# A table held in two float32r parts instead of three bf16 parts, with shared places for the 0/1 tiles, in the attention pass of a graph network kernel

## The chip, the core and the metric

The kernel is one launch on one NeuronCore of a Trainium2 chip. The metric is device time of the whole launch in microseconds. A difference of about 0.5% (some 98 us) is what a measurement of this kernel can tell from no change.

## The reference, cut to what matters

Four graph layers follow each other on 6250 nodes and 200000 edges. The edges are sorted by `dst`. The second layer is the one the change is in: for each edge it looks up the rows of both ends, makes one attention number of them, and sums and takes the maximum of the weighted rows over the edges of each node.

```python
row, col = (edge_index[0], edge_index[1])          # src, dst
ef = edge_label @ trans_weight
node_feat = x[row] * x[col]
att = jax.nn.sigmoid(_leaky_relu(node_feat @ attention_weight) + _leaky_relu(ef @ edge_attention_weight))
wef = ef * att
wnf = x[col] * att
wsf = x[row] * att
...
s = jax.ops.segment_sum(vals, idx, num_segments=n)
mx = jax.ops.segment_max(vals, idx, num_segments=n)
```

## The kernel before, in words

All engines are programmed by hand with semaphores; there is no scheduler. Edges lie as 128 partitions times 1568 places, and a pass walks over them in blocks of B = 16 places (2048 edges). A loop of IT = 49 turns handles two such blocks, called halves: `h` is 0 or 1, `n = 2 * i + h` counts them, and buffers that come in pairs are indexed by `h`. So the attention pass (`attention_pass`, lines 1143 to 1487) does 98 halves.

In each half the row `x[src]` of 16 x 128 edges is needed. Ten of the sixteen come by indirect DMA from the DRAM table `att_table` into `rows[h]` (POOL, L1263). The other K = 6 are looked up on TensorE: the table of 6272 nodes, 65 numbers each, stands in SBUF as 128 partitions x 7 classes (`WIDE_CLASSES`) x 455 columns. `one_lo[h]` is a 0/1 tile that says in which partition and class an edge's node is, made by VectorE from `keys[h]` in `one_hots` (L1367, 7 instructions for 7 classes of 768 columns). For each of the six places TensorE multiplies the table's 7 classes by that 0/1 tile and adds up in PSUM (`multiply`, L1341). Because the 0/1 tile and the table are bf16, the float32 table is split in three bf16 parts whose sum is the number: 7 classes x 3 parts = 21 matmuls of 455 columns for a place, 42 for one call of `multiply(h, g)`, which does two places (G = 3 groups g = 0, 1, 2). VectorE then picks the right one of 7 slots in `pick(g)` (L1404) and adds up in `gather(g)` (L1407).

The order in a half `n` is written out:

- TensorE: `multiply(h, 0)` after pick 1 of half n - 1, `multiply(h, 1)` after pick 2 of half n - 1, the label products (L1357), `multiply(h, 2)` after pick 0 of half n. There are two PSUM tiles `p_slots`, used in turn.
- VectorE: pick 0, the 0/1 tiles of the next half (`one_hots`, `one_slots`), gather 0, the 16-step chain that completes `xdst` (L1427), pick 1, label score, gather 1, pick 2, gather 2, product with `x[dst]` and reduction to the score (L1446 to L1457), rows for the attention (L1461, L1462), then `chains` for the half before (L1383, L1385): 16 steps of running sums and running maxima in `run`.
- ScalarE: sigmoid of the score (L1326), then three times 16 weighted rows (L1302): first `out_rows`, then two parts of `msg`.
- POOL: 16 scatters of `out_rows` to the DRAM tensor `sent` (`scatter`, L1272) when VectorE and ScalarE have made them, and behind them in the same queue the 10 gathers of a later half (`gather`, L1263). The order is gather of half n + 1, scatter of n, gather of n + 2, scatter of n + 1. So after each scatter of half n come the gathers of half n + 2.
- SyncE: loads of `xdst`, labels and keys for later halves, and the store of `run` to `running_dst` (`store_last`, L1224).

Ahead of the pass the table is split by `split_wide` (L852, L854) on VectorE while POOL scatters `begun_x` (L1133). The last layer (`softmax_pass`, L1630) has the same kind of lookup, but from a table in two float32r parts, with `e_one_lo` tiles in float32r (L1777 and L1800); it is not changed. Lines below are those of the kernel before.

## Time and profile before

| | us |
|---|---|
| median of 3 runs | 19641.05 (19631.51 to 19712.04) |
| span of the profiled execution | 19593.6 |
| first and last sigmoid of the attention pass | 5940.0 and 10831.2 |
| PE busy in the span | 11895.5 (61%) |
| DVE busy | 10634.3 (54%) |
| POOL busy | 9080.8 (46%) |
| ACT busy | 4354.8 (22%) |

The profile is one execution. PE is TensorE's matmul, PEld its weight load, DVE VectorE, ACT ScalarE, POOL GpSimd, SP SyncE. "Idle before" is time in which an engine stood idle just ahead of an instruction; "issue" as its reason means that the engine waited for nothing that the profile shows. No engine is busy all the time: the attention pass, about a quarter of the span, has to be read by what follows what.

### The profile page before, as it was taken

How to read it: one execution, taken by the hardware profiler on the slowest of the kernel's cores; microseconds unless marked ns; L12 is line 12 of the kernel's file. 1: busy time of each engine (PE TensorE's matmuls, PEld its weight loads, DVE VectorE, ACT ScalarE, POOL GpSimd, SP SyncE). 2: the span in 40 equal slices, each digit the busy share in tenths (PEclk: the TensorE clock that was granted, in tenths of full speed). 3: DMA queues.
4: the chain of work that ended last, by engine and by line, in shares of the span. 5: the costliest groups of instructions: out<-in, count | busy, mean ns of one | idle time of the engine just before them, and what ended most of it. 6: DMA issues, size and time to landing. Idle time of an engine off the chain costs nothing. (4 is left out here: it accounts for less than half of the span.)

```text
span 19593.6 us, 235897 instructions
## 1 busy us (share of the span) xinstructions
PE 11895.5 (61%) x70205; PEld 7895.5 (40%) x70205; DVE 10634.3 (54%) x24515; ACT 4354.8 (22%) x14847; POOL 9080.8 (46%) x9348
## 2 busy tenths in 40 slices
PE   4444445555546666666666446776776777566664
PEld 3333334444432222222222115665664333355453
DVE  5555545555544545555545794554554555356565
ACT  2333322333312222222222330000000111022221
POOL 4444434444445455455455103555444555444444
PEclk7777767777767777777777667887887888678777
DMA  2111112222212222222222671111111111022221
GB/s 62 58 58 58 58 48 75 77 76 76 77 55 64 69 65 70 69 65 70 69 65 70 214 260 31 32 32 29 31 32 29 34 34 34 23 56 57 58 56 48
DMA packets 637409, 1245.55 MB, mean 64 GB/s; under 512 B 206034, under 2 KB 390391, under 8 KB 586531
## 3 DMA queue, kind: packets, MB, share of 16 engines
q1 hardware_dynamic: 322624, 912.21, 13.3%
q0 software_dynamic: 300160, 269.02, 7.8%
q10 hardware_dynamic: 14337, 61.82, 0.8%
q14 instruction: 270, 2.20, 0.0%
q8 instruction: 18, 0.29, 0.0%
HBM read 475.84 MB, written 768.08 MB: 63 GB/s over the span
## 5 line engine op out<-in xcount | busy, mean ns | idle before, releaser
L1030 PE MATMUL p_slots<-part,one_lo 128*128 128x208 bf16 (+1 forms) x27048 | 3678.2, 296 | 1143.2 <-issue 992.4
L1341 PE MATMUL a_p_slots<-att_part,a_one_lo 128*128 128x455 bf16 x12348 | 2986.2, 389 | 1868.8 <-issue 1782.6
L1030 PEld LDWEIGHTS p_slots<-part,one_lo 128*128 128x128 bf16 x27048 | 2663.8, 105 | 2157.5 <-issue 1446.8
L990 POOL DMA_INDIRECT rows<-gcn_table,index x2450 | 2384.7, 973 | 2462.5 <-DVE p_msg L1109 1507.9
L1341 PEld LDWEIGHTS a_p_slots<-att_part,a_one_lo 128*128 128x128 bf16 x12348 | 1254.1, 102 | 3623.5 <-issue 2574.9
L1272 POOL DMA_INDIRECT sent<-a_out_rows,a_place x1568 | 1543.2, 984 | 2165.6 <-DVE a_run L1383 1688.3
L556 POOL DMA_INDIRECT msg<-x_rows,index x1372 | 1310.7, 955 | 1431.8 <-ACT index L574 1020.1
L1078 DVE TENSOR_TENSOR picked<-p_slots,one_hi 128x832 f32<-128x832 f32 (+1 forms) x588 | 708.2, 1204 | 2280.1 <-remote 1825.8
L556 POOL DMA_INDIRECT msg<-h_rows,index x1274 | 1225.8, 962 | 1533.0 <-ACT index L574 1174.2
L622 PE MATMUL p_slots<-x_part,key_lo 128*128 128x448 f32 x6916 | 1859.9, 429 | 121.6 <-DVE scratch L751 71.5
L1777 PE MATMUL e_p_slots<-soft_part,e_one_lo 128*128 128x456 f32 x5488 | 1429.0, 410 | 745.7 <-issue 674.4
L1734 POOL DMA_INDIRECT e_rows<-soft_table,e_index x1176 | 1140.6, 970 | 1157.1 <-DVE e_p_msg L1890 797.3
L622 PEld LDWEIGHTS p_slots<-x_part,key_lo 128*128 128x128 f32 x6916 | 1557.8, 232 | 273.0 <-DVE scratch L751 88.2
L788 DVE SCALAR_TENSOR_TENSOR run<-run,keep,msg 128x129 f32<-128x129 f32 (+1 forms) x3136 | 1112.8, 355 | 976.4 <-ACT msg L591 779.0
L1777 PEld LDWEIGHTS e_p_slots<-soft_part,e_one_lo 128*128 128x128 f32 x5488 | 1142.2, 212 | 997.1 <-issue 790.9
L1404 DVE TENSOR_TENSOR a_picked<-a_p_slots,a_one_hi 128x910 f32<-128x910 f32 x294 | 324.9, 1105 | 2080.4 <-remote 1043.7
L1018 ACT ACTIVATE run_rows<-run 128x256 f32<-128x256 f32 (+1 forms) x294 | 230.5, 784 | 4158.4 <-DVE run L1113 4023.3
L1263 POOL DMA_INDIRECT a_rows<-att_table,a_index x980 | 959.3, 979 | 305.6 <-issue 298.4
L658 PE MATMUL p_look<-one_hi,earlier 128*128 128x49 bf16 x3920 | 331.8, 187 | 864.3 <-issue 862.7
L1326 ACT ACTIVATE a_att<-a_score 128x16 f32<-128x16 f32 x98 | 21.2, 216 | 3616.2 <-DVE a_score L1457 3616.2
L584 ACT ACTIVATE earlier<-p_same 128x1280 bf16<-128x1280 f32 x392 | 484.9, 1237 | 1397.7 <-remote 761.8
L635 PE MATMUL p_same<-not_earlier,ident_b 128*128 128x512 bf16 x392 | 195.5, 499 | 961.6 <-ACT final L578 872.2
(479 smaller groups left out, 18270.4 us busy)
## 6 DMA issues: line engine op xcount, KB each, us to landing
running_dst<-a_run SPq DMA_DIRECT2D x98, 1600.0 KB
running_src<-s_run SPq DMA_DIRECT2D x98, 1600.0 KB
running<-run SPq DMA_DIRECT2D x98, 1032.0 KB
running<-run SPq DMA_DIRECT2D x98, 1024.0 KB
running<-y SPq DMA_DIRECT2D x98, 656.0 KB
s_rows<-sent ACTq DMA_DIRECT2D x98, 584.0 KB
begun_x<-zeros SPq DMA_DIRECT2D x98, 512.0 KB
a_xdst<-begun_x SPq DMA_DIRECT2D x98, 512.0 KB
```

Of the source, the lines that this page charges most:

```text
L556: pool.indirect_dma_start(out=msg[h][:, K + k, 0:C], out_offset=None, in_=table, in_offset=offsets(index[h][:, k:k + 1])).then_inc(gathere ...
L584: nc.scalar.activation(flat(earlier[q][:]), flat(p_same[:, 0:PAIRS, :]), ACT.Relu).then_inc(same_sb, 1)
L622: ins = nc.tensor.matmul(p_slots[:, bank, 0:C * WIDE_CLASS], key_lo[h][:, c, e:e + P], flat(part[:, c, :, :]), start=c == 0 and part_no == ...
L788: step(nc.vector.scalar_tensor_tensor(run[h][:, k, :], before, keep[h][:, k:k + 1], msg[h][:, k, :], ALU.mult, ALU.add))
L990: pool.indirect_dma_start(out=rows[h][:, KS[h] + k, :], out_offset=None, in_=table, in_offset=offsets(index[h][:, k:k + 1])).then_inc(gath ...
L1030: ins = nc.tensor.matmul(to, one_lo[h][:, q, e:e + P], flat(part[:, q, :, :]), start=q == 0 and part_no == 0, stop=q == CLASSES - 1 and pa ...
L1078: step(nc.vector.tensor_tensor(picked[g][:, 0:many, :, :], slots(g, many), mask, ALU.mult))
L1263: pool.indirect_dma_start(out=rows[h][:, K + k, :], out_offset=None, in_=table, in_offset=offsets(index[h][:, k:k + 1])).then_inc(gathered ...
L1272: pool.indirect_dma_start(out=sent, out_offset=offsets(place[h][:, k:k + 1]), in_=out_rows[h][:, k, :], in_offset=None).then_inc(scattered ...
L1341: ins = nc.tensor.matmul(to[:, k, 0:Z * WIDE_CLASS], one_lo[h][:, q, e:e + P], flat(part[:, q, :, :]), start=q == 0 and part_no == 0, stop ...
L1734: pool.indirect_dma_start(out=rows[h][:, KS[h] + k, :], out_offset=None, in_=table, in_offset=offsets(index[h][:, k:k + 1])).then_inc(gath ...
L1777: ins = nc.tensor.matmul(p_slots[g][:, k, 0:WIDE_COLUMNS], one_lo[h][:, q, e:e + P], part[:, q, :], start=q == 0 and part_no == 0, stop=q ...
```

## The change

Everything is in the attention pass and its table.

1. The table stands in two float32r parts instead of three bf16 parts. `multiply` issues 7 x 2 = 14 matmuls for a place instead of 21, of 456 columns (one column of padding) instead of 455. The columns, PSUM tiles, waits and their order are as before.
2. The 0/1 tile `one_lo` is float32r, so it takes twice the space. The tiles of both halves lie in one tile in which the last third of half 0's and the first third of half 1's are the same place. So that this place is free in time, half 0 now does its groups in another order (columns 4 and 5 first, then 0 and 1, then 2 and 3), given by the new function `columns(h, g)`.
3. `run` is one buffer instead of two. The first step of a chain reads the last row of the same buffer, and a chain now waits for the store of the chain just before it instead of the one before that.
4. `picked` and `label_part` lie in `scratch` (the tile `y`) behind `product`.

```diff
@@ attention_pass
-        one_lo, one_hi = pair("a_one_lo", [P, WIDE_CLASSES, K * P], BF16), pair("a_one_hi", [P, K, WIDE_CLASS])
-        picked = [sb(f"a_picked{g}", [P, K // G, Z, WIDE_CLASS]) for g in range(2)]
+        LATE = (K - K // G) * P
+        one_lo_all = sb("a_one_lo", [P, WIDE_CLASSES, LATE + K // G * P + LATE], F32R)
+        one_lo = [one_lo_all[:, :, 0:K * P], one_lo_all[:, :, LATE:LATE + K * P]]
+        one_hi = pair("a_one_hi", [P, K, WIDE_CLASS])
+        PICKED = K // G * Z * WIDE_CLASS
...
-        out_rows, msg, run = pair("a_out_rows", [P, B, SENT]), pair("a_msg", [P, B, WIDE]), pair("a_run", [P, B, RUN])
+        out_rows, msg, run = pair("a_out_rows", [P, B, SENT]), pair("a_msg", [P, B, WIDE]), sb("a_run", [P, B, RUN])
...
+        def columns(h, g):
+
+            first = g * (K // G) if h else (g - 1) % G * (K // G)
+            return slice(first, first + K // G)
...
-                sp.dma_start(running_v[:, bass.ds((n - 1) * B, B), :], run[1 - h][:]).then_inc(stored[1 - h], 16)
+                sp.dma_start(running_v[:, bass.ds((n - 1) * B, B), :], run[:]).then_inc(stored[1 - h], 16)
...
-                    e = (g * (K // G) + k) * P
+                    e = (columns(h, g).start + k) * P
                     for q in range(WIDE_CLASSES):
                         for part_no, part in enumerate(parts):
-                            ins = nc.tensor.matmul(to[:, k, 0:Z * WIDE_CLASS], one_lo[h][:, q, e:e + P], flat(part[:, q, :, :]),
+                            ins = nc.tensor.matmul(to[:, k, 0:WIDE_COLUMNS], one_lo[h][:, q, e:e + P], part[:, q, :],
...
-                    before = run[b][:, k - 1, :] if k else run[1 - b][:, B - 1, :]
+                    before = run[:, (k - 1) % B, :]
...
-                        cut = slice(g * (K // G), (g + 1) * (K // G))
+                        cut = columns(h, g)
...
-                        dve.wait_ge(stored[1 - h], 16 * (i + h))
+                        dve.wait_ge(stored[h], 16 * (i + 1))
                         chains(1 - h, step, after)
...
@@ gnn
-            parts = [sb(f"att_part{n}", [P, WIDE_CLASSES, C + 1, WIDE_CLASS], BF16, wide) for n in range(3)]
+            parts = [sb(f"att_part{n}", [P, WIDE_CLASSES, WIDE_COLUMNS], F32R, wide) for n in range(2)]
```

TensorE's stream at the head of the loop, before: half 0's groups 0 and 1, the labels, group 2, then half 1's groups 0 and 1. "x42" is 42 matmuls in a row.

```order
L1341 MATMUL a_p_slots<-att_part,a_one_lo 128x455 x42
L1350 REGISTER_ALU
L1341 MATMUL a_p_slots<-att_part,a_one_lo 128x455 x42
L1353 ISA
L1354 REGISTER_ALU
L1357 MATMUL a_p_label<-w_labels,a_label 128x512 x2
L1360 ISA
L1341 MATMUL a_p_slots<-att_part,a_one_lo 128x455 x42
L1350 REGISTER_ALU
L1341 MATMUL a_p_slots<-att_part,a_one_lo 128x455 x42
```

The same place in the changed kernel:

```order
L1351 MATMUL a_p_slots<-att_part,a_one_lo 128x456 x28
L1360 REGISTER_ALU
L1351 MATMUL a_p_slots<-att_part,a_one_lo 128x456 x28
L1363 ISA
L1364 REGISTER_ALU
L1367 MATMUL a_p_label<-w_labels,a_label 128x512 x2
L1370 ISA
L1351 MATMUL a_p_slots<-att_part,a_one_lo 128x456 x28
L1360 REGISTER_ALU
L1351 MATMUL a_p_slots<-att_part,a_one_lo 128x456 x28
```

Nothing has moved; each run of 42 matmuls is one of 28.

VectorE at the start of the chain that stands at the end of half 1 (it sums half 0's messages), before:

```order
L1461 TENSOR_TENSOR a_out_rows<-a_label_row,a_att 128x16x8 [waits a_activated]
L1462 TENSOR_TENSOR a_msg<-a_label_row,a_att 128x16x8
L1383 SCALAR_TENSOR_TENSOR a_run<-a_run,a_keep,a_msg 128x72 [waits a_stepped,a_stored0,a_label_made]
L1385 SCALAR_TENSOR_TENSOR a_run<-a_run,a_pen,a_msg 128x128 [waits a_stepped]
L1383 SCALAR_TENSOR_TENSOR a_run<-a_run,a_keep,a_msg 128x72 [waits a_stepped]
```

and after:

```order
L1471 TENSOR_TENSOR a_out_rows<-a_label_row,a_att 128x16x8 [waits a_activated]
L1472 TENSOR_TENSOR a_msg<-a_label_row,a_att 128x16x8
L1393 SCALAR_TENSOR_TENSOR a_run<-a_run,a_keep,a_msg 128x72 [waits a_stepped,a_stored1,a_label_made]
L1395 SCALAR_TENSOR_TENSOR a_run<-a_run,a_pen,a_msg 128x128 [waits a_stepped]
L1393 SCALAR_TENSOR_TENSOR a_run<-a_run,a_keep,a_msg 128x72 [waits a_stepped]
```

The instructions are the same; the first one waits for the other store semaphore, that of the chain just before.

## Rows read from the trace of the kernel before

**Rows 1.** Page, costliest groups: line, engine, tiles, count | busy us, mean ns | idle before, releaser.
```profile
L1341 PE MATMUL a_p_slots<-att_part,a_one_lo 128*128 128x455 bf16 x12348 | 2986.2, 389 | 1868.8 <-issue 1782.6
L1272 POOL DMA_INDIRECT sent<-a_out_rows,a_place x1568 | 1543.2, 984 | 2165.6 <-DVE a_run L1383 1688.3
L1263 POOL DMA_INDIRECT a_rows<-att_table,a_index x980 | 959.3, 979 | 305.6 <-issue 298.4
```

**Rows 2.** Line L1326, the sigmoid: count, duration, first and last start.
```profile
L1326 ACT ACTIVATE a_att<-a_score x98: 215/216/218, 5940.0 to 10831.2; 128x16 f32<-128x16 f32 x98
```

**Rows 3.** Timeline, PE: start us, us, instruction, count [idle before].
```profile
8810.10 20.94 PE L1341 MATMUL a_p_slots<-att_part,a_one_lo 128*128 128x455 bf16 x97 [0.19 <-issue]
...
8832.59 5.02 PE L1341 MATMUL a_p_slots<-att_part,a_one_lo 128*128 128x455 bf16 x25
8837.98 0.36 PE L1341 MATMUL a_p_slots<-att_part,a_one_lo 128*128 128x455 bf16 x1 [0.37 <-issue]
...
8861.90 18.71 PE L1341 MATMUL a_p_slots<-att_part,a_one_lo 128*128 128x455 bf16 x87 [0.86 <-issue]
```

**Rows 4.** Timeline, POOL: first scatter, last gather, next first scatter.
```profile
8825.12 1.12 POOL L1272 DMA_INDIRECT sent<-a_out_rows,a_place  x1 [18.99 <-DVE a_run L1383]
...
8858.03 0.95 POOL L1263 DMA_INDIRECT a_rows<-att_table,a_index  x1 [0.30 <-issue]
...
8873.50 1.00 POOL L1272 DMA_INDIRECT sent<-a_out_rows,a_place  x1 [14.52 <-DVE a_run L1383]
```

**Rows 5.** Timeline, DVE and ACT, between pick 0 and the next pick 0.
```profile
8831.30 1.11 DVE L1404 TENSOR_TENSOR a_picked<-a_p_slots,a_one_hi 128x910 f32<-128x910 f32 x1 [2.85 <-issue]
8836.06 2.40 DVE L1367 TENSOR_SCALAR a_one_lo<-a_keys,lanes 128x768 bf16<-128x768 f16 x7 [3.66 <-issue]
...
8844.50 1.10 DVE L1404 TENSOR_TENSOR a_picked<-a_p_slots,a_one_hi 128x910 f32<-128x910 f32 x1
...
8863.23 1.11 DVE L1404 TENSOR_TENSOR a_picked<-a_p_slots,a_one_hi 128x910 f32<-128x910 f32 x1 [15.02 <-PE a_p_slots L1341]
...
8868.72 3.93 ACT L1302 ACTIVATE a_out_rows<-a_xdst,a_att 128x64 f32<-128x64 f32 x16
...
8877.07 1.10 DVE L1404 TENSOR_TENSOR a_picked<-a_p_slots,a_one_hi 128x910 f32<-128x910 f32 x1
```

**Rows 6.** Timeline near the pass's start, PE and POOL: a stretch without POOL work.
```profile
5926.35 24.47 PE L1341 MATMUL a_p_slots<-att_part,a_one_lo 128*128 128x455 bf16 x126
...
5944.99 1.15 POOL L1272 DMA_INDIRECT sent<-a_out_rows,a_place  x1 [29.45 <-DVE a_one_lo L1367]
```

**Rows 7.** Windows: stretch, its length, PE, PEld, DVE, ACT, POOL busy, PEclk, DMA.
```profile
8838.00:8860.00 22.00, 6.53 (x13) 1.41 (x14) 9.68 (x26) 0.00 (x0) 16.14 (x16) 0.58 0.16 36
...
8862.50:8865.00 2.50, 2.50 (x8) 0.99 (x7) 1.74 (x2) 0.00 (x0) 0.00 (x0) 0.50 0.00 0
8865.00:8867.50 2.50, 2.50 (x13) 1.15 (x12) 2.43 (x3) 0.00 (x0) 0.00 (x0) 0.90 0.00 0
```

**Rows 8.** Timeline of the last layer, PE and POOL, two halves of gathers without a break.
```profile
18014.16 6.07 PE L1777 MATMUL e_p_slots<-soft_part,e_one_lo 128*128 128x456 f32 x28
...
18029.49 3.86 PE L1777 MATMUL e_p_slots<-soft_part,e_one_lo 128*128 128x456 f32 x11
18034.52 0.38 PE L1777 MATMUL e_p_slots<-soft_part,e_one_lo 128*128 128x456 f32 x1 [1.16 <-issue]
...
18014.38 0.95 POOL L1734 DMA_INDIRECT e_rows<-soft_table,e_index  x1 [16.74 <-DVE e_p_msg L1890]
...
18043.71 0.95 POOL L1734 DMA_INDIRECT e_rows<-soft_table,e_index  x1 [0.30 <-issue]
```

**Rows 9.** Timeline of the last layer, DVE: 0/1 tiles in float32r.
```profile
18003.27 2.85 DVE L1800 TENSOR_SCALAR e_one_lo<-e_keys,lanes 128x512 fp32r<-128x512 f16 x7
```

**Rows 10.** Timeline, DVE, its first instruction in the attention pass.
```profile
5889.55 0.12 DVE L1372 MEMSET a_run<- 128x72 f32 x1 [40.80 <-PEq L2307]
```

More of the change, by code:

```diff
@@ L1176, in attention_pass @@
         keys = pair("a_keys", [P, K * P], F16)
-        one_lo, one_hi = pair("a_one_lo", [P, WIDE_CLASSES, K * P], BF16), pair("a_one_hi", [P, K, WIDE_CLASS])
-        picked = [sb(f"a_picked{g}", [P, K // G, Z, WIDE_CLASS]) for g in range(2)]
+        LATE = (K - K // G) * P
[3 more added lines that the diff above has]
+        PICKED = K // G * Z * WIDE_CLASS
+        picked = [scratch[:, B * C + g * PICKED:B * C + (g + 1) * PICKED].rearrange("p (k c s) -> p k c s", k=K // G, s=WIDE_CLASS) for g in range(2)]
         rows, xdst = pair("a_rows", [P, B, Z]), pair("a_xdst", [P, B, C])
@@ L1380, in chains @@
                 for k in range(B):
-                    before = run[b][:, k - 1, :] if k else run[1 - b][:, B - 1, :]
+                    before = run[:, (k - 1) % B, :]
                     after(1 if k else 0)
-                    step(nc.vector.scalar_tensor_tensor(run[b][:, k, 0:SUMS], before[:, 0:SUMS], keep[b][:, k:k + 1], msg[b][:, k, 0:SUMS], ALU.mult, ALU.add))
+                    step(nc.vector.scalar_tensor_tensor(run[:, k, 0:SUMS], before[:, 0:SUMS], keep[b][:, k:k + 1], msg[b][:, k, 0:SUMS], ALU.mult, ALU.add))
                     after(1)
-                    step(nc.vector.scalar_tensor_tensor(run[b][:, k, SUMS:RUN], before[:, SUMS:RUN], pen[b][:, k:k + 1], msg[b][:, k, LABELS:WIDE], ALU.add, ALU.max))
+                    step(nc.vector.scalar_tensor_tensor(run[:, k, SUMS:RUN], before[:, SUMS:RUN], pen[b][:, k:k + 1], msg[b][:, k, LABELS:WIDE], ALU.add, ALU.max))
             def both_halves(i, first):
@@ L1403, in pick @@
                         dve.wait_ge(looked, G * n + g + 1)
-                        step(nc.vector.tensor_tensor(picked[g % 2][:], slots, mask, ALU.mult))
+                        step(nc.vector.tensor_tensor(picked[g % 2], slots, mask, ALU.mult))
                     def gather(g):
-                        step(nc.vector.tensor_reduce(rows[h][:, g * (K // G):(g + 1) * (K // G), :], picked[g % 2][:], AX.X, ALU.add))
+                        step(nc.vector.tensor_reduce(rows[h][:, columns(h, g), :], picked[g % 2], AX.X, ALU.add))
                     dve.wait_ge(staged, n + 1)
@@ L1431, in both_halves @@
                     assert done[0] == SECOND_MADE
-                    step(nc.vector.tensor_tensor(label_part[:], label_row[h][:], repeat(w_label_att, B), ALU.mult))
+                    step(nc.vector.tensor_tensor(label_part, label_row[h][:], repeat(w_label_att, B), ALU.mult))
                     after(1)
@@ L1435, in both_halves @@
                     after(1)
-                    step(nc.vector.tensor_reduce(label_score[:], label_part[:], AX.X, ALU.add))
+                    step(nc.vector.tensor_reduce(label_score[:], label_part, AX.X, ALU.add))
                     step(nc.vector.tensor_tensor(product[:], xdst[h][:], repeat(w_att, B), ALU.mult))
@@ L1476, in _ @@
             dve.wait_ge(label_made, 2 * IT + 2)
-            dve.wait_ge(stored[1], 16 * IT)
+            dve.wait_ge(stored[0], 16 * (IT + 1))
             made = [INIT + per * 2 * IT]
@@ L1486, in _ @@
             dve.wait_ge(stepped, INIT + per * (2 * IT + 1))
-            nc.vector.tensor_copy(final[:], run[1][:, B - 1, :]).then_inc(stepped, 1)
+            nc.vector.tensor_copy(final[:], run[:, B - 1, :]).then_inc(stepped, 1)
 def source_pass(nc, sig, block, ctx, sent, w_labels, running, final, zeros):
```

7 lines of the change are left out of this document (4 added, 3 removed).

## The prediction

> **What bounds the kernel now.** I read the page's costliest groups first. In the attention pass no engine is full, and two rows stand out: 12348 matmuls of L1341 with 1868.8 us of idle before them, of which 1782.6 have no reason that the profile shows ("issue"), and 1568 scatters of L1272 with 2165.6 us of idle, most of it until VectorE is done [rows 1]. Then the sigmoid's line: 97 intervals between 5940.0 and 10831.2, so 50.4 us for a half [rows 2]. Then the timeline of one half, engine by engine.
>
> TensorE runs in two ways. From 8862 on it does 87 matmuls in 18.71 us, and from 8832.59 25 in 5.02 us, 0.20 us each. Then, from 8837.98, the same instructions come one at a time: of the 42 matmuls of this group the last 3 are in the next row, so 14 take the 24 us up to 8861.90, 1.7 us each, though nothing is waited for [rows 3]. In that stretch the granted clock is 0.58 on average, and PE has 13 matmuls in 22 us [rows 7]. So the slow stretch isn't arithmetic; matmuls are supplied slowly.
>
> When? POOL issues 26 indirect DMAs without a break from 8825.12 to 8858.98. The slow stretch begins 12.5 us after the first and ends 2.9 us after the last one's end [rows 3, 4]. Where POOL stood still, before 5944.99, TensorE did 126 matmuls in 24.47 us without a gap [rows 6]. The last layer says more. There POOL's gathers of two halves run on without a break from 18014.38 to 18044.66; TensorE still does 28, 28, 2 and 11 matmuls (first and last of the four rows are shown), and from 18034.52 it crawls too [rows 8]. From the start of POOL's burst that is 69 matmuls in 19 us there; here about 30 of the 97-matmul row, 4 passes for the labels and 25, so 59 in 12.5 us [rows 3, 4]. Times differ, counts are alike. My reading: **while POOL issues indirect DMAs, TensorE lives on some 60 to 69 matmuls' worth of instructions that it has in store, and then gets one matmul in about 1.7 us until 3 to 4 us after POOL's last.**
>
> The ring that sets the pace: group 2 is done at 8863.2, so pick 2 starts at 8863.23, then score, sigmoid, 16 weighted rows from 8868.72 for 3.93 us, and the next burst at 8873.50, 10.3 us after pick 2 [rows 4, 5]. Burst (34 us), end of the slow stretch and rest of group 2 (4.2), 10.3: 48.4 us. The other kind of half, in which VectorE starts pick 0 only at 8831.30 after 2.85 us of "issue" and the 0/1 tiles at 8836.06 after 3.66 more, is later [rows 5]; the mean is 50.4.
>
> **The change, part by part.**
>
> *Matmuls, 42 to 28 a group.* A half has 84 instead of 126 plus the labels' 4 passes. The price of one in float32r with 456 columns is in the last layer: 28 in 6.07 us, 0.217 us, against 0.20 [rows 3, 8]. At the low clock both take 0.38 us (455 or 456 columns at 1.2 GHz; the row of 2.50 us with 8 matmuls at 0.50 is near that [rows 7]). So a group costs 6.1 instead of 8.2 us. What counts more is the store. At a burst's start (10.3 us after pick 2) groups 0 and 1 of the next half have run for 10.3 us: 9 matmuls at the low clock in 3.4 us [rows 7], the rest at 0.217, so some 42 of 56. Left until the end of group 2: 14, 4 passes, 28 = 46, under 59. **So group 2 now ends inside the burst, before the slow stretch begins**, about 12 us in: pick 0 is free at about +4.7 us (8877.07 + 1.1 against 8873.50 [rows 4, 5]), and 28 matmuls take 6.1.
>
> *What is late next in that half.* Then VectorE: one_hots, gather 0, the chain on `xdst`, pick 1, and pick 2 about 3.7 us behind it. From 8836.06 to 8844.50 is 8.4 us before pick 1 [rows 5]; with the dearer 0/1 tiles (below) 9.8. So pick 1 starts near +14.5, pick 2 near +18.2, and the next scatter could start at +28.5. POOL isn't ready before 26 x 1.28 us (984 and 979 ns each plus 0.30 of issue [rows 1, 4]) = 33.3 us. So the next scatter follows at once (with the two stalls of 6.5 us it would be 2 us late): **two bursts merge to 66.6 us**, in which TensorE is starved only once.
>
> *The second half of such a pair.* Its groups 0 and 1 fall in the merged burst. From +16 us (pick 1 done) the remaining 59 - 46 = 13 come fast, until about +19; from there to the end of the slow stretch (66.6 + 3.5 = 70 us) it is 51 us at 1.7 us each, 30 matmuls. So 43 of 56 are done at 70 us. Left: 13, 4 passes, 28. First 3.4 us at the low clock, 9; then 32 at 0.217 us, 6.9; the labels 1.7: 12.0 us. Then 10.3 us from pick 2 to the next burst. Pair: 70.1 + 12.0 + 10.3 = 92.4 us, **46.2 us for a half, 4.2 less than 50.4**. Times 98: 412 us.
>
> *0/1 tiles in float32r.* 7 instructions of 768 columns took 2.40 us [rows 5]; in float32r 7 of 512 take 2.85 us [rows 9]. For 768 that is at least 2.85 and at most, in proportion, 4.3; I take 3.8, nearer to the upper, since most of an instruction goes with its columns. 1.4 us more a half, before pick 1. In the first half of a pair POOL's queue hides it (+28.5 against +33.3); in the second, pick 1 waits for TensorE. So 0; uncovered it would be 137 us.
>
> *One buffer of running sums.* The chain now waits for the store begun after the chain before. Queued behind that wait on VectorE are pick 0 and the 0/1 tiles of the next half. The store is issued as the chain ends (near 8828.6) and the next chain starts 40 us later; in a merged burst 30 us at least. From 8838 on the DMA engines are 0.16 busy [rows 7], so it has landed within 10 us. Cost 0.
>
> *Shared places, other order of columns.* Pick 0 frees the shared third before the 0/1 tiles are written, and that order was there already. No wait is added. The move of `picked` and `label_part` adds none either. 0.
>
> *Splitting the table.* Two large VectorE instructions fewer, two small ones more. VectorE then stands idle for 40.80 us until the pass begins [rows 10], so 0 is gained.
>
> **Sum.** 19593.6 - 412 = 19182 for the profiled execution. The median before is 47 us above its span, so 19229; I give **19230 us**.
>
> *A rule weighed against the rows.* The Trainium skill, "Runtime: NRT & Kernel Launch", section "Instruction fetch mechanics", has TensorE's instructions kept in a store that is refilled ahead, with the fetch hidden behind execution. The rows of the slow stretch speak against "hidden". By that rule the slow stretch would be due to POOL's burst as such and not to a count.
>
> **Rivals.**
>
> *A. Slow by time, not by count (unmerged).* If TensorE is slow from 12 us on after a burst's start whatever it has used, or the store is smaller than 46 (it holds 59 by one place, but the count is taken with the engine at full pace), group 2 doesn't end before the crawl. For it: in this pass the stretch always begins after about 12 us. Against: 19 us in the last layer [rows 8]. Then every half keeps its ring: 33.3 + 3.5 + 1 (few matmuls left) + 10.3 = 48.1 us, 2.3 less: 225 us, 19415. The skill's rule would lead here.
>
> *B. POOL becomes the bound.* If 28-matmul groups never starve, a half is 33.3 us and the gain 17.1 x 98 = 1676 us: 17965. Against: the last layer has groups as small and crawls [rows 8].
>
> *C. Slower: VectorE starves in the merged burst.* VectorE issues about 75 instructions and as many register steps a half, and has shown stalls of 2.85 and 3.66 us with no cause inside a burst [rows 5]. Nothing here shows it in 66 us of POOL work. If it has a store like TensorE's, it is late in the second half: after the slow stretch it still has the chain of 16 steps (7.5 us from 8869.3 to pick 0 at 8877.07), pick 0, tiles, `xdst` chain, pick 1 (11) and 3.7 to pick 2, and only then the 10.3. Pair: 70.1 + 7.5 + 11 + 3.7 + 10.3 = 102.6, 51.3 a half: 88 us slower; with the two stalls of 6.5 us on the path too, 54.6: 412 us slower, 20053. I price it midway, 52.9 a half, 245 us, 19886. It makes the kernel slower if more than 20 us of VectorE's work is left at +70 (70.1 + 20.4 + 10.3 is twice 50.4).
>
> *D. No change.* The pair merges, but the crawl is nearer 2.2 us a matmul, as in the last layer (from 18034.52 on 7 in some 15 us), and VectorE is partly late. 7 matmuls more (1.5 us) and 6 us: 99.9 us a pair, 50.0 a half: 19602.
>
> **How the numbers follow.** Forecast 0.60, A 0.15, B 0.06, C 0.08, D 0.11. Within the forecast the bounds are: a store of 69 instead of 59 (10 matmuls fewer left, 2.2 us a pair), no time at the low clock (1.5), merged bursts that also save the other half's delay; together with a faster crawl (1.2 us each: 12 more matmuls, 2.6 us) down to 85 us a pair, 18870. Upwards the 2 us of delay, a loop branch in the burst that empties the store (13 more left, 3 us) and the crawl at 2.2: 97 us, 19450. A lies within. Those two alone hold 0.75, so the range reaches to D: 18850 to 19610 leaves out B, C and the tails, under 0.2. For the forecast alone it would be 18870 to 19450. The measurement can't tell less than 0.5%, 98 us, from no change: faster 0.82 (forecast, A, B), same 0.10, slower 0.08.
>
> **What would show it.** Right: scatter starts that alternate, one with 0.3 us of idle before it, the next some 22 us after POOL's last gather; intervals of the sigmoid alternating near 33 and 59 us; "issue" before the lookup matmuls well below 1782.6 us; one_lo near 540 ns each. Wrong: scatters with equal idle before every burst (A), none at all (B), or VectorE with gaps of 0.7 us without a wait in the second burst (C). The chain's first step should show no wait for the store.

## The result, and the profile after

| | before | after |
|---|---|---|
| median of four runs, us | 19636.28 | 19134.72 |
| lowest and highest, us | 19602.48 to 19712.04 | 19106.69 to 19176.47 |
| profiled execution's span, us | 19593.6 | 19105.0 |

The ratio is 0.9739, with a 95% interval of 0.9724 to 0.9753 (the two medians alone give 0.9745). The change made the kernel 2.6% faster. Here and below a ratio goes by a kernel's fast executions alone, which matters only for three_places_wait, where two of four are left out as slow. Forecast were 19230 us and a range of 18850 to 19610.

The lines of the page that answer to [rows 1], line numbers moved by about 10, and the line of the sigmoid that answers to [rows 2]:

```profile
L1351 PE MATMUL a_p_slots<-att_part,a_one_lo 128*128 128x456 f32 x8232 | 2379.7, 452 | 1771.9 <-DVE y L1414 875.5
L1282 POOL DMA_INDIRECT sent<-a_out_rows,a_place x1568 | 1569.1, 1001 | 1640.7 <-DVE a_run L1393 1158.6
```
```profile
L1336 ACT ACTIVATE a_att<-a_score x98: 215/216/218, 5946.8 to 10337.5; 128x16 f32<-128x16 f32 x98
```

A half takes (10337.5 - 5946.8) / 97 = 45.3 us instead of 50.4. The 97 intervals add up to 500.5 us less and the span is 488.6 less, so the whole gain is in this pass. POOL's idle time before its scatters fell by 525 us. That agrees. TensorE's idle time hardly fell (1868.8 to 1771.9 us), but its reasons changed: the longer view of the same row has 794.6 us of "issue", where [rows 1] has 1782.6:

```profile
L1351 PE MATMUL a_p_slots<-att_part,a_one_lo 128*128 128x456 f32 x8232 | 2379.7, 452 | 1771.9 <-DVE y L1414 875.5 <-issue 794.6 <-DVE a_one_lo L1377 81.3
```

How a half gets its length is seen on three engines. First POOL's timeline, the first scatter of a burst, its last gather and the first scatter of the next (columns as in [rows 4]):

```profile
8313.00 1.00 POOL L1282 DMA_INDIRECT sent<-a_out_rows,a_place  x1 [14.16 <-DVE a_run L1393]
...
8345.42 0.95 POOL L1273 DMA_INDIRECT a_rows<-att_table,a_index  x1 [0.30 <-issue]
8359.29 1.01 POOL L1282 DMA_INDIRECT sent<-a_out_rows,a_place  x1 [12.92 <-DVE a_run L1393]
```

Then TensorE in the same burst: group 2, then group 0 of the next half.

```profile
8317.74 7.62 PE L1351 MATMUL a_p_slots<-att_part,a_one_lo 128*128 128x456 f32 x28 [2.28 <-DVE y L1414]
8329.26 6.77 PE L1351 MATMUL a_p_slots<-att_part,a_one_lo 128*128 128x456 f32 x23 [3.90 <-issue]
8337.10 0.37 PE L1351 MATMUL a_p_slots<-att_part,a_one_lo 128*128 128x456 f32 x1 [1.07 <-issue]
8339.20 0.45 PE L1351 MATMUL a_p_slots<-att_part,a_one_lo 128*128 128x456 f32 x1 [1.73 <-issue]
```

And VectorE: pick 0 and the 0/1 tiles, pick 1, its last instruction ahead of pick 2, and pick 2:

```profile
8316.58 1.11 DVE L1414 TENSOR_TENSOR y<-a_p_slots,a_one_hi 128x910 f32<-128x910 f32 x1
8317.60 4.39 DVE L1377 TENSOR_SCALAR a_one_lo<-a_keys,lanes 128x768 fp32r<-128x768 f16 x7
...
8328.11 1.10 DVE L1414 TENSOR_TENSOR y<-a_p_slots,a_one_hi 128x910 f32<-128x910 f32 x1
...
8331.66 0.17 DVE L1449 SCALAR_TENSOR_TENSOR a_label_score<-a_label_score 128x16 f32<-128x16 f32 x1
8349.03 1.10 DVE L1414 TENSOR_TENSOR y<-a_p_slots,a_one_hi 128x910 f32<-128x910 f32 x1 [17.20 <-remote]
```

Group 2 is done at 8325.4, 12.4 us after the burst's start. VectorE has nothing left but pick 2 from 8331.8 on, 18.8 us after it. Yet pick 2 starts at 8349.03, with 17.20 us of "remote" before it (the profile found no instruction that ended just before the wait did). POOL's last gather ended at 8346.4. The semaphore record that TensorE's last matmul of group 2 leaves is not at 8325.4 either: it stands at 8349.01, and that of the group behind it at 8349.93, though that one ran until 8346.0. So **the signal was late, not the work**. It isn't this half alone: over 95 halves of after, pick 2 starts 21.6 us (median) behind the end of its group's last matmul, and in 89 of them a semaphore record stands at its start. In the trace of one_run (below), where nothing is starved, the record stands 0.01 us behind the matmul in every half. Not every signal leaves a record (282 for 294 groups in after), so a record alone wouldn't show it; pick 2's start beside it does. (The profile models a matmul's end; but group 0, behind group 2 in TensorE's order, starts at 8329.26, so group 2's matmuls were at least all under way by then.) In the other direction nothing is late: pick 1 starts at 8328.11 and takes 1.10 us, and TensorE starts group 0 at 8329.26, inside the burst.

Three intervals, read from the starts and ends of all halves but the first two and the last (medians, us; here and below a half is the mean):

| | last gather's end to pick 2 | pick 2 to the next scatter | half |
|---|---|---|---|
| before | 7.5 | 10.3 | 50.4 |
| after | 3.1 | 10.3 | 45.3 |

The commonest half of after is 33.4 (POOL's burst) + 3.2 + 10.3 = 46.9 us. In 22 of 95 halves pick 2 started before the burst's end; there the signal wasn't held to the end, and the half is shorter. Why the signal passed earlier in those the trace doesn't show.

### The profile page after: what moved, and what is told of

It reads as the page before. It is cut to its first block and busy times, and to the rows that moved or that the text cites. A ratio compares the mean times of both kernels' runs of the same rounds, so it can differ in the third digit from the quotient of the medians.

```text
span 19105.0 us, 227665 instructions
## 1 busy us (share of the span) xinstructions
PE 11353.8 (59%) x66089; PEld 8604.7 (45%) x66089; DVE 10805.0 (57%) x24515; ACT 4357.6 (23%) x14847; POOL 9086.6 (48%) x9348
## 5 line engine op out<-in xcount | busy, mean ns | idle before, releaser
L1351 PE MATMUL a_p_slots<-att_part,a_one_lo 128*128 128x456 f32 x8232 | 2379.7, 452 | 1771.9 <-DVE y L1414 875.5
L1351 PEld LDWEIGHTS a_p_slots<-att_part,a_one_lo 128*128 128x128 f32 x8232 | 1962.8, 242 | 2246.6 <-DVE y L1414 1030.2
L1414 DVE TENSOR_TENSOR y<-a_p_slots,a_one_hi 128x910 f32<-128x910 f32 x294 | 324.4, 1103 | 1403.8 <-remote 1138.9
L794 DVE TENSOR_TENSOR seen_lo<-p_sums,seen_hi 128x49 bf16<-128x49 f32 x392 | 81.9, 209 | 1255.5 <-ACT seen_hi L587 1255.5
L591 ACT ACTIVATE msg<-msg,weight 128x64 f32<-128x64 f32 x3136 | 767.3, 336 | 3.7 <-DVE msg L769 3.7
```

The costliest lines, as they stand in the source:

```text
L591: nc.scalar.activation(msg[h][:, k, C:2 * C], msg[h][:, k, 0:C], ACT.Copy, scale=weight[h][:, k:k + 1]).then_inc(weighed, 1)
L1351: ins = nc.tensor.matmul(to[:, k, 0:WIDE_COLUMNS], one_lo[h][:, q, e:e + P], part[:, q, :], start=q == 0 and part_no == 0, stop=q == WIDE_ ...
```

## Experiments

The kernels of one batch ran on the same chip, and each is compared with the kernel before in that batch. That matters here: in five batches the kernel before took 19610 to 19950 us, in two batches 13486 and 13511 us. The same chip was of both kinds in different batches. I call them "starved" and "unstarved"; no trace that I read says what differs, only what follows from it.

**Two parts in bf16.** The kernel before, with 28 matmuls a group. It leaves the table's third part out, so its output is another one; the places of its sent rows are made of row numbers that POOL writes ahead of the pass (the lines with `rank`):

```diff
+                used = parts[:2]
...
-                        for part_no, part in enumerate(parts):
+                        for part_no, part in enumerate(used):
...
-                    step(nc.vector.tensor_tensor(place[h][:], rows[h][:, :, C], rank[h][:], ALU.add))
+                    step(nc.vector.scalar_tensor_tensor(place[h][:], rows[h][:, :, C], 0.0, rank[h][:], ALU.mult, ALU.add))
...
+                    pool.iota(rank[:, 0:T], [[1, T]], base=0, channel_multiplier=T, allow_small_or_imprecise_dtypes=True).then_inc(pool_s.sem, 1)
```

> The kernel before with 28 bf16 matmuls a group instead of 42: the third part of the table is left out, and the place of a sent row is the row's own number instead of the looked-up start plus its rank. It has neither float32r nor the shared places. Halves are between sigmoids of the attention pass: 50.4 us before, 45.3 after. Theory 'count' (the gain is from fewer TensorE instructions in a half, whatever their type): 45 to 46 us a half, about 19130 us, and 0/1 tiles at 2.4 us for 7. If it comes to 1 us a half less than after (19030), the dearer 0/1 tiles of the float32r version (4.35 us for 7) are on the path. Rival 'float32r' (the wide type itself brings the gain): near 50 us a half, 19600.

**Three parts in float32r.** The kernel after, with 14 matmuls more a group:

```diff
+                    for q in range(WIDE_CLASSES):
+                        nc.tensor.matmul(to[:, k, 0:WIDE_COLUMNS], one_lo[h][:, q, e:e + P], parts[1][:, q, :], start=q == 0, stop=q == WIDE_CLASSES - 1)
                     for q in range(WIDE_CLASSES):
                         for part_no, part in enumerate(parts):
```

> The kernel after with 14 float32r matmuls more in every group, 42 in all as before, into the same PSUM places and then overwritten; the output is unchanged. Theory 'count': TensorE crawls again in POOL's burst as before, 50 to 52 us a half (19600 to 19800), with 'issue' before the lookups back near 1780 us. Rival 'float32r': 45 to 47 us a half, 19130 to 19300.

**One part.** The kernel after, with `used = parts[:1]` and the same edits of `place` and `rank`: 14 matmuls a group. It leaves the second part out; its output is another one too, and its rows are sent to other places.

> The kernel after with one part of the table instead of two, 14 matmuls a group (the second part is left out; the place of a sent row is the row's own number instead of the looked-up start plus its rank). In the kernel after, group 2 ends 12 us after the burst's start, but VectorE learns of it only 2.6 us after the burst's end. Theory 'held by time' (TensorE's signals reach nobody until POOL's 26 indirect DMAs are issued): group 2 ends earlier still, pick 2 starts as late: a half stays 46 to 47 us, 19130 to 19250. Theory 'held by place' (TensorE's signals stand in a row that moves by one matmul in about 1.5 us during the burst, so the last of 4 + 14 passes at 27 us, not the 32nd at 48): pick 2 some 25 to 28 us after the burst's start and a half of 36 to 40 us, 18200 to 18600. The prediction's theory (store and crawl, no held signals): never starved, POOL the bound, 33.3 us a half, 17965.

**One buffer of running sums**, alone, in the kernel before:

```diff
-        out_rows, msg, run = pair("a_out_rows", [P, B, SENT]), pair("a_msg", [P, B, WIDE]), pair("a_run", [P, B, RUN])
+        out_rows, msg, run = pair("a_out_rows", [P, B, SENT]), pair("a_msg", [P, B, WIDE]), sb("a_run", [P, B, RUN])
...
-                        dve.wait_ge(stored[1 - h], 16 * (i + h))
+                        dve.wait_ge(stored[h], 16 * (i + 1))
```

> The kernel before with one buffer of running sums and nothing else of the change. The chain then waits for the store of the chain before it. In the kernel after, no idle time before the chain's first step is put down to that store. Every theory: 50.4 us a half, 19636 within 0.3%. If the store were late under bf16's order of work, 1 us of wait a half would make 100 us more.

Measured, in a batch in which the kernel before took 13486.47 us:

| | ratio to before | 95% interval | us a half |
|---|---|---|---|
| two_parts_bf16 | 1.0019 | 1.0009 to 1.0028 | 34.2 |
| three_f32r | 1.0037 | 1.0023 to 1.0051 | 34.4 |
| one_part | 1.0018 | 1.0008 to 1.0028 | 34.4 |
| one_run | 1.0000 | 0.9990 to 1.0009 | 34.0 |

None of the expectations on TensorE was met: in this batch TensorE had no slow stretches to shorten. The page and the sigmoid of one_run, which has the 42 matmuls and the order of the kernel before:

```profile
L1341 PE MATMUL a_p_slots<-att_part,a_one_lo 128*128 128x455 bf16 x12348 | 2550.0, 370 | 400.7 <-DVE a_picked L1404 321.1
L1272 POOL DMA_INDIRECT sent<-a_out_rows,a_place x1568 | 1582.6, 1009 | 496.8 <-issue 462.8
```
```profile
L1326 ACT ACTIVATE a_att<-a_score x98: 215/216/218, 3901.1 to 7200.7; 128x16 f32<-128x16 f32 x98
```

TensorE has no "issue" among its reasons (the 400.7 us are 321.1 of this one and 79.6 of the 0/1 tiles, L1370), where [rows 1] has 1782.6 us of it. POOL's scatter takes as long as there (1009 against 984 ns), and its idle time is mostly its own 0.30 us per DMA. So an unstarved half is POOL's 26 DMAs, 34 us, whether a group has 14, 28 or 42 matmuls. It is rival B's mechanism (33.3 us), in a setting that the trace of before didn't show. One buffer of running sums costs nothing there. In the starved trace of after, the waits for its store are 5.8 us in the whole pass, on line L1393:

```profile
L1393 DVE SCALAR_TENSOR_TENSOR a_run<-a_run,a_keep,a_msg 128x72 f32<-128x72 f32 x1568 | 451.6, 288 | 24.8 <-DVE a_run L1395 10.0 <-DMA running_dst<-a_run 5.8 <-issue 2.5
```

**The changed kernel once more.**

> The changed kernel once more, because in the runs before this one the kernel before took 13486 us instead of 19636 us and no half of the attention pass had a slow stretch (34.0 us a half with one buffer of running sums). Theory 'count with slow stretch' (the change gains only by what TensorE loses while POOL issues indirect DMAs): where the kernel before takes about 13486 us, POOL's 26 DMAs set the half (34 us) in both kernels, and the changed one takes 13486 us within 0.5%; where the kernel before takes about 19636 us, the changed one takes about 19130 us. Rival 'less work is less time' (14 matmuls fewer a group are 9 us of TensorE a half): 13000 us or less beside 13486.

This batch was starved: before 19941.54, this 19519.88 us, ratio 0.9805 (0.9736 to 0.9873), 46.6 us a half. There is a gain again, of 1.3 to 2.6% by the interval, which overlaps the first; by itself this batch doesn't tell whether it reaches 2%. In 5 of 95 halves the signal came early, against 22 of 95. The changed kernel itself was not run in an unstarved batch; there its neighbours with 14 and 42 float32r matmuls stood at 1.002 and 1.004.

**One part, starved.**

> The kernel of one_part once more, for a chip on which TensorE has its slow stretches (where the kernel before takes some 19600 to 19950 us); where it takes some 13490 us, every theory gives 13490 us, since POOL's 26 DMAs set the half there. On the slow kind: 'held by time' (TensorE's signals reach nobody until 2.6 us after POOL's burst): a half stays 46 to 47 us, 0.974 to 0.98 of before. 'Held by place' (the signals stand in a row that moves by one matmul in about 1.5 us during the burst, and the last matmul of group 2 is now the 18th in it and no longer the 32nd): pick 2 some 25 to 28 us after the burst's start and a half of 36 to 40 us, 0.93 to 0.95 of before. The prediction's theory (store and crawl, no signal is held): POOL is the bound, 33.3 us a half, 0.91 to 0.92.

Measured: before 19855.23, this 19356.99 us, ratio 0.9766 (0.9696 to 0.9837), 45.8 us a half. The total is what "held by time" expected, the mechanism is not. TensorE and VectorE, then POOL, in two bursts that follow each other:

```profile
7992.34 3.50 PE L1352 MATMUL a_p_slots<-att_part,a_one_lo 128*128 128x456 f32 x14 [0.45 <-issue]
8003.84 4.51 PE L1352 MATMUL a_p_slots<-att_part,a_one_lo 128*128 128x456 f32 x14 [8.00 <-issue]
...
8002.68 1.10 DVE L1415 TENSOR_TENSOR y<-a_p_slots,a_one_hi 128x910 f32<-128x910 f32 x1
...
8007.02 1.11 DVE L1415 TENSOR_TENSOR y<-a_p_slots,a_one_hi 128x910 f32<-128x910 f32 x1
...
8035.04 0.39 DVE L1396 SCALAR_TENSOR_TENSOR a_run<-a_run,a_pen,a_msg 128x128 f32<-128x128 f32 x1 [0.42 <-DVE a_run L1394]
8036.45 0.29 DVE L1394 SCALAR_TENSOR_TENSOR a_run<-a_run,a_keep,a_msg 128x72 f32<-128x72 f32 x1 [1.02 <-DVE a_run L1396]
8037.85 0.35 DVE L1396 SCALAR_TENSOR_TENSOR a_run<-a_run,a_pen,a_msg 128x128 f32<-128x128 f32 x1 [1.10 <-DVE a_run L1394]
8052.05 1.11 DVE L1415 TENSOR_TENSOR y<-a_p_slots,a_one_hi 128x910 f32<-128x910 f32 x1 [13.84 <-remote]
```
```profile
7987.58 1.01 POOL L1282 DMA_INDIRECT sent<-a_out_rows,a_place  x1 [22.43 <-DVE a_run L1394]
...
8024.87 0.98 POOL L1282 DMA_INDIRECT sent<-a_out_rows,a_place  x1 [2.89 <-issue]
```

Group 2 is done at 7995.8, the 18th matmul of the burst (4 for the labels, 14). Pick 2 follows at 8007.02 with no wait, 19.4 us after the burst's start and some 14 us before its end. So a burst doesn't hold every signal; "held by time" falls. "Held by place" had pick 2 at 25 to 28 us and 36 to 40 us a half; neither came. In after the signal held was that of the 32nd (4 and 28); that the place in the burst decides isn't shown. And now the bursts do follow each other almost without a break (the second starts 37.3 us after the first), and in the second VectorE itself issues an instruction only every 0.7 to 1.4 us from 8033 on. Then it stands 13.84 us before the pick at 8052.05, the next half's pick 0, whose matmuls had ended at 8008.4 (the row at 8003.84). The profile says "remote" there, but before 46 other picks 0 it says "issue", 499.6 us in all or 10.9 each, where before has 2.9:

```profile
L1415 DVE TENSOR_TENSOR y<-a_p_slots,a_one_hi 128x910 f32<-128x910 f32 x294 | 323.8, 1101 | 538.1 <-issue 499.6 <-remote 32.0 <-DVE a_label_score L1477 0.2
```

So it isn't TensorE's work that VectorE waits for there; I read it as VectorE short of its own instructions. Sigmoids mostly come 31 to 36 and 47 to 69 us apart in turn. That is the alternation of the forecast and the starving VectorE of rival C. The time that the first half of a pair wins, the second gives back.

**Three PSUM places.** The kernel after, with every group of half n + 1 one pick earlier (group 0 behind pick 0 and the 0/1 tiles of half n, group 1 behind pick 1, group 2 behind pick 2), and with POOL's scatters waiting for the signals of all three, so that they are out before the burst:

```diff
-        p_slots = [ctx.enter_context(nc.psum_tensor(f"a_p_slots{g}", [P, K // G, 512], F32)) for g in range(2)]
-        p_label = [ctx.enter_context(nc.psum_tensor(f"a_p_label{h}", [P, B, C], F32)) for h in range(2)]
+        p_slots = [ctx.enter_context(nc.psum_tensor(f"a_p_slots{g}", [P, K // G, 512], F32)) for g in range(G)]
+        p_label = ctx.enter_context(nc.psum_tensor("a_p_label", [P, B, C], F32))
...
-                    for g, free in enumerate((SECOND_MADE, THIRD_MADE)):
+                    for g, free in enumerate((ONE_HOTS, SECOND_MADE, THIRD_MADE)):
...
-                    pe.wait_ge(stepped, INIT + per * n + 1)
-                    multiply(h, 2)
...
                 pool.wait_ge(stepped, INIT + per * (2 * i + h) + PLACED)
+                if not last:
+                    pool.wait_ge(looked, G * (2 * i + h + 2))
```

> The kernel after with three PSUM places for the lookups' groups instead of two (and one instead of two for the labels), so that group 2 of the next half runs right behind pick 2, and with POOL's scatter waiting until TensorE's signal for that group is out, so that no pick of the next half waits for a signal that POOL's burst holds. On a chip with slow stretches, both held-signal theories: the pick-2 wait inside the burst goes; what is left is TensorE's count, 88 matmuls a half, of which the store gives 59 in a burst; burst 33.4, end of the slow stretch 3, 29 matmuls at 0.217 us 6.3: 42.7 us a half against 45.3 to 46.6, 0.955 to 0.965 of before. If no signal is held and only the supply of matmuls counts, the same 42.7 is the most it can be and the kernel after should have been there already. If the wait costs more than it frees: 47 to 50 us a half, 0.98 to 1.0. On a chip without slow stretches POOL's wait is satisfied before its scatter is ready, 34 us a half, 13490 us.

Measured: 18802.22 beside 19855.23 us, ratio 0.9394 (0.9323 to 0.9465), 40.3 us a half. The ratio rests on the faster two of four executions (18600.84 and 18713.8 us); the medians of all give 0.947, and the profiled execution, 18898.0 us, 0.952. It computes the same output and is faster than both kernels: some 2.3 to 3.5% below the changed one's 0.9739, in another batch, intervals apart. POOL's first scatters of two bursts, and VectorE's picks 0, 1 and 2 of one half and pick 0 of the next:

```profile
8018.11 1.30 POOL L1284 DMA_INDIRECT sent<-a_out_rows,a_place  x1 [11.41 <-PE a_p_slots L1353]
...
8056.82 1.29 POOL L1284 DMA_INDIRECT sent<-a_out_rows,a_place  x1 [3.92 <-remote]
```
```profile
8013.73 1.11 DVE L1413 TENSOR_TENSOR y<-a_p_slots,a_one_hi 128x910 f32<-128x910 f32 x1
...
8024.59 1.10 DVE L1413 TENSOR_TENSOR y<-a_p_slots,a_one_hi 128x910 f32<-128x910 f32 x1
...
8028.22 1.10 DVE L1413 TENSOR_TENSOR y<-a_p_slots,a_one_hi 128x910 f32<-128x910 f32 x1
...
8050.13 1.11 DVE L1413 TENSOR_TENSOR y<-a_p_slots,a_one_hi 128x910 f32<-128x910 f32 x1 [4.64 <-issue]
```

Pick 2 at 8028.22 lies in the middle of the burst and waits for nothing, with the same 28 matmuls a group as after. The edit is worth some 5 us a half (45.3 and 46.6 against 40.3). It moves the groups' work and makes POOL wait besides taking the signals out of the burst's way; three places without POOL's wait were not run, so the 5 us aren't split. But group 2's work was no longer what a half of after waited for, only its signal. "No signal is held, only the supply counts" had said that the kernel after would have been there already; it falls. It came out 2.4 us under the 42.7 of the held-signal theories: in the burst at 8018 TensorE did 84 lookup matmuls without a slow stretch, not 59, and 41 of 95 bursts had none.

**The two controls and a pause.** two_parts_bf16_slow and three_f32r_slow repeat the first kernels; three_places_pause adds to the last:

```diff
                 scatter(0, i)
+                pool.wait_ge(scattered[0], 16 * B * (i + 1))
                 gather(0, i + 1)
                 scatter(1, i)
+                pool.wait_ge(scattered[1], 16 * B * (i + 1))
```

> The kernel of two_parts_bf16 (28 bf16 matmuls a group, nothing else of the change) once more, for a chip with slow stretches, where the changed kernel came to 0.974 and 0.981 of before and 45.3 and 46.6 us a half. Theory 'count' (fewer TensorE instructions in a half, whatever their type): 45 to 47 us a half, 0.97 to 0.98. Rival 'float32r' (its longer weight loads, 197 against 102 ns, give the instructions more time each to be supplied): near 50 us a half, 0.99 to 1.0. On a chip without slow stretches, 1.002 as before.

> The kernel of three_f32r (the changed kernel with 42 float32r matmuls a group, output unchanged) once more, for a chip with slow stretches. Theory 'count': group 2 isn't done before the slow stretch begins, so 50 to 53 us a half and 1.0 to 1.02 of before. Rival 'float32r': 45 to 47 us a half, 0.97 to 0.98. Rival 'signals only' (TensorE's count doesn't matter, only that its signals are late behind a burst): 47 to 48 us a half, 0.98. On a chip without slow stretches, 1.004 as before.

> The kernel of three_places_wait (40.3 us a half, 0.939 of before) with a pause in POOL's burst: behind its 16 scatters it waits until the last of them has landed, about 2.6 us, before it issues the 10 gathers. Theory 'a burst wears down a store that a pause fills': bursts of 20.5 and 12.8 us are each too short to starve TensorE and VectorE, so POOL is the bound at 33.4 + 2.6 and the wait for group 2, 36 to 38 us a half, 0.91 to 0.93. Rival 'the pause is too short, the slow stretch ends 2.6 to 4 us after POOL's last': nothing is filled and the pause adds itself, 42 to 43 us, 0.95 to 0.96.

The batch was unstarved (before 13511.45 us): 1.0003 (0.9993 to 1.0012), 1.0022 (1.0013 to 1.0032) and 1.0175 (1.0158 to 1.0192). The last took 36.7 us a half, 2.3 more than the 34.4 of three_f32r; three_places_wait, which it should be set against, was not run in an unstarved batch, so that 2.3 is the pause alone is taken, not shown. 28 matmuls in bf16 were not run in a starved batch, so that they alone would do as well isn't shown. The next run goes the other way: it undoes the count and keeps float32r.

**Three parts in float32r, starved.**

> The kernel of three_f32r (the changed kernel with 42 float32r matmuls a group, output unchanged) once more, since the run before this one was again on a chip where the kernel before takes some 13500 us; there 1.002 to 1.004 is expected again. On a chip with slow stretches (before some 19600 to 19950 us): theory 'count': group 2 isn't done before the slow stretch begins, so 50 to 53 us a half and 1.0 to 1.02 of before. Rival 'float32r': 45 to 47 us a half, 0.97 to 0.98. Rival 'signals only' (TensorE's count doesn't matter, only that its signals are late behind a burst): 47 to 48 us a half, 0.98.

Measured: before 19871.31, this 19970.6 us, ratio 1.0055 (1.0028 to 1.0081), 51.8 us a half. Of the three theories "count" is right. Nothing of the change but the number of matmuls was undone, and the whole gain went. (Undoing it gives back the instructions and TensorE's time for them together; the two weren't separated.) Its page:

```profile
L1353 PE MATMUL a_p_slots<-att_part,a_one_lo 128*128 128x456 f32 x8232 | 2077.7, 397 | 789.9 <-issue 789.4
L1350 PE MATMUL a_p_slots<-att_part,a_one_lo 128*128 128x456 f32 x4116 | 1205.4, 411 | 1116.9 <-issue 1035.6
```

"Issue" is back at 789.4 + 1035.6 = 1825 us ([rows 1]: 1782.6). Pick 2 starts 8.8 us after the last gather, and pick 2 to scatter is 10.3 again. "Signals only" (48 us) falls: in this kernel group 2's matmuls themselves are late.

**The pause, starved.**

> The kernel of three_places_pause once more; on the chip of its first run, where the kernel before takes some 13500 us, it was 1.0175 of before, and that is expected there again. On a chip with slow stretches, where three_places_wait had 40.3 us a half and 0.939 of before: theory 'a burst wears down a store that a pause fills': bursts of 20.5 and 12.8 us are each too short to starve TensorE and VectorE, 36 to 38 us a half, 0.91 to 0.93. Rival 'the pause is too short, the slow stretch ends 2.6 to 4 us after POOL's last': nothing is filled and the pause adds itself, 42 to 43 us, 0.95 to 0.96.

Measured: before 19613.52, this 18650.49 us, ratio 0.9502 (0.9479 to 0.9525), 40.7 us a half. No store is filled in a pause of some 3 us. TensorE goes on one at a time right through one (POOL ended its scatters at 8046.7 and started its gathers at 8049.16):

```profile
8044.12 0.54 PE L1355 MATMUL a_p_slots<-att_part,a_one_lo 128*128 128x456 f32 x1 [2.26 <-issue]
8046.22 0.54 PE L1355 MATMUL a_p_slots<-att_part,a_one_lo 128*128 128x456 f32 x1 [1.57 <-issue]
8049.03 0.54 PE L1355 MATMUL a_p_slots<-att_part,a_one_lo 128*128 128x456 f32 x1 [2.27 <-issue]
8050.45 0.54 PE L1355 MATMUL a_p_slots<-att_part,a_one_lo 128*128 128x456 f32 x1 [0.88 <-issue]
```
```profile
8045.71 1.01 POOL L1284 DMA_INDIRECT sent<-a_out_rows,a_place  x1 [0.31 <-issue]
8049.16 0.98 POOL L1273 DMA_INDIRECT a_rows<-att_table,a_index  x1 [2.45 <-issue]
```

By the two traces the pause cost 0.4 us a half (40.7 against 40.3) and not 2.3: the bursts grew by 2.3 us (mean 33.9 to 36.2), and POOL's idle time between them shrank by 1.9 (6.4 to 4.6). By the ratios (0.9502 against 0.9394, of two batches) it would be 1.1%, 2.2 us a half. Which of the two holds stays open. The rival's ratio (0.95 to 0.96) came out at its lower end; its 42 to 43 us a half were too many. That a store is filled in the pause falls by either.

## Why the prediction was right, point by point

*Fewer matmuls, 0.217 us each; group 2 ends before the slow stretch, 12 us in.* Right: 12.4 us. That there is no gain without the lower count is shown by three_f32r_again; that the count alone is enough, without float32r, no starved run shows.

*The store of 59 to 69 and the crawl.* The count is right for these kernels, somewhat smaller. Read from all bursts but the first two and the last, the matmuls (labels included) from a burst's start until two in a row come with 0.5 us or more of idle before them, and the time until then (medians):

| | matmuls, middle 80% of bursts | us | bursts with a slow stretch |
|---|---|---|---|
| before | 55, 52 to 58 | 12.9 | 95 of 95 |
| after | 58, 55 to 65 | 25.5 | 69 of 95 |
| three_f32r_again | 54, 52 to 58 | 13.7 | 95 of 95 |
| three_places_wait | 70, 53 to 81 | 20.2 | 54 of 95 |

Between before and after the time doubles and the count stays, so rival A's "slow from 12 us on whatever it has used" is out. three_places_wait doesn't fit a fixed count either, and POOL's pause before a burst doesn't explain it: the burst at 8018 with its 84 came after one of 11.4 us, the burst of after at 8313 with its 55 after one of 14.2. The crawl's pace was too fast: 2.1 us a matmul in after (four intervals from 8337.10 to 8345.50), and 2.15 over the bursts of before itself; the 1.7 was that of one half.

*VectorE ready for pick 2 at +18.2.* It was ready at +18.8.

***Pick 2 at +18.2, next scatter at +28.5, two bursts merge.*** This is the step that failed. It took the end of a matmul for the moment at which VectorE knows of it, and so put nothing for the signal. Pick 2 came at +36.0, and no burst of after followed another at once. The sign named for the merge, scatters in turn with 0.3 and some 22 us of idle, isn't there: 14.16, then 12.92. The evidence was in the page of before, in the row of the picks, which I had not used:

```profile
L1404 DVE TENSOR_TENSOR a_picked<-a_p_slots,a_one_hi 128x910 f32<-128x910 f32 x294 | 324.9, 1105 | 2080.4 <-remote 1043.7
```

Half of the picks' idle time is put down not to TensorE's matmuls but to "remote"; I took all of it for unfinished work. Nearly all of that half (959.7 us, 59 times) stands before pick 1. Pick 1 and pick 2 of the half before the one in [rows 5]:

```profile
8805.88 1.11 DVE L1404 TENSOR_TENSOR a_picked<-a_p_slots,a_one_hi 128x910 f32<-128x910 f32 x1 [19.29 <-remote]
...
8814.87 1.10 DVE L1404 TENSOR_TENSOR a_picked<-a_p_slots,a_one_hi 128x910 f32<-128x910 f32 x1 [5.26 <-PE a_p_slots L1341]
```

Pick 1's group had ended at 8779.4, 26.5 us earlier. So the kernel before already had late signals. There they cost nothing: pick 2 still had to wait for group 2's matmuls (5.26 us here; in 95 of 98 halves its wait ended with them). Once those end early, in after, the late signal sets the half. The merging, and what it does to the second half, are real where the signal isn't late: one_part_slow.

*46.2 us a half, 412 us.* Measured 45.3 and 500. The size is right by another ring, and so by luck: burst 33.4, 3.2 until the signal, 10.3 from pick 2 to the scatter. That is rival A's ring with 3.2 in place of its 3.5 + 1, for another cause; A was priced at 48.1 and given 0.15. What brings the mean below the ring's 46.9 are the 22 halves with an early signal. So the time was forecast well and its cause only half: the first half of the pair's argument (fewer matmuls end the wait for work) held, the second (what is late next) named the wrong thing.

*0/1 tiles 3.8 us.* Measured 4.39, just over the upper bound of 4.3 (691 ns each over the pass, not 540); that is 1.95 us a half more VectorE time. It is hidden in VectorE's 17 us of waiting, as said, and cover is left.

*Run buffer, shared places, table split: 0.* one_run 1.0000, 5.8 us of waits in all. The others have no row in the trace that names them, and weren't tried alone.

*Rival B* is the unstarved setting. *Rival C's* sign, VectorE with gaps of 0.7 us without a cause, is there in one_part_slow and, milder, in three_places_wait; in after VectorE has done its work before it would starve. The stalls of 2.85 and 3.66 us that C took as its first sign are none, though: they come once a loop's turn, and in the unstarved one_run they are as long (before pick 0 137.9 us in 47 turns, against 136.4 in before). *Rival D* priced the crawl right (2.2) and had the rest wrong.

*The rule of the skill.* The row first: between [rows 1] and one_run the "issue" of the same matmuls goes from 1782.6 us to nothing, while the profile's instruction queue moves the same amount (kernel before, starved, then one_run, unstarved; packets, MB, share):

```profile
q14 instruction: 270, 2.20, 0.0%
```
```profile
q14 instruction: 269, 2.20, 0.1%
```

The Trainium skill, "Runtime: NRT & Kernel Launch", section "Instruction fetch mechanics", says that the fetch is mostly hidden behind execution and that a taken branch outside the fetched pages stalls. The unstarved runs agree with "hidden". As far as this queue counts the fetches, there are no more of them in the starved ones, which speaks against refetching; and a packet takes as long (mean 0.42 us in before, 0.43 in one_run). That a fetch is held up before it starts isn't excluded.

**What stays open.** What makes a batch starved, and what the thing is that runs short while POOL issues indirect DMAs. It slows TensorE's matmuls, its signals and VectorE's instructions, which points to something the engines share; no run shows what. Which signals are late and why 22 halves had an early one stays open too, and whether 28 matmuls in bf16 would have given the same gain.

## What to carry to other kernels

The end of a matmul in a timeline isn't yet the start of whoever waits for it: where a wait shows "remote" and the producer had long been done, look for the semaphore's own record, and set the order so that the signal is out before the other engine's burst begins (here another 2.3 to 3.5%). Before costing a stall of the kind "issue", see whether a second batch has it at all: here the same program took 13.5 or 19.6 ms, 31% less without them. Fewer instructions on a starved engine help only until the next shared thing is late: 42 to 28 matmuls gave 2.6%, 28 to 14 nothing that can be told from it (0.977 of before, against 0.974 and 0.981).

## What the runs showed of the hardware that I had not expected

- The same kernel took 13486 to 13511 us in two batches and 19610 to 19950 in five; one and the same chip was among both, with a scatter nearly as long (1009 and 984 ns).
- In starved batches TensorE's signal of a finished group was seen 23.6 us after the matmul's end (8325.4 to 8349.0; median over the halves of after 21.6), 2.6 us after the end of POOL's last indirect DMA, against 0.01 us in one_run; that of the 18th matmul of a burst was there in at most 11.2 us (7995.8 to 8007.0). VectorE's signals to TensorE weren't late (1.15 us).
- In a second burst behind the first, VectorE also issues only one small instruction in 0.7 to 1.4 us.
- In a starved batch TensorE's slow stretch begins after some 55 matmuls of POOL's burst, be that 12.9 us (before) or 25.5 us (after) into it. A break of 2.5 us in the burst doesn't end it.
- VectorE stands 2.9 us before the first pick of each loop's turn with no reason shown, starved or not.
- 7 instructions from f16 to float32r, 768 columns each, take 4.39 us on VectorE, against 2.40 to bf16 [rows 5].
